# Local attention layers: the sum over the probabilities one place later on VectorE, and PSUM slots given out by expected release

## The reference

```python
for i in range(6):
    x = attn_layer(shift_tokens(x), Wqkv[i], q_scale[i], k_scale[i], Wo[i]) + x
    x = ffn_layer(shift_tokens(x), ln_g[i], ln_b[i], W1[i], b1[i], W2[i], b2[i]) + x
# attn_layer: 16 heads of 64; q, k = l2norm(q) * qs, l2norm(k) * ksc, rotary with a decay;
#   each window of 32 queries attends to its own and the previous 32 keys:
sim = where(mask, -max, einsum('bhwie,bhwje->bhwij', bq, bk2) * 8)
attn = softmax(sim, -1); out = attn @ v; out = out @ Wo
# ffn_layer: layer norm, hg = xn @ W1 + b1; a, gate = split(hg); (a * gelu(gate)) @ W2 + b2
```

## Time and profile before

| | us |
|---|---|
| median of 3 runs | 4151.44 |
| lowest and highest run | 4146.84, 4154.14 |
| the profiled execution, its own time | 4158.42 |
| its span in the trace | 4156.6 |
| stage of the local layers in the trace | 2440 to about 3420 |

### The profile page before, as it was taken

The page is one execution under the profiler, slowest core; times in us unless marked ns, Lnnn a source line. Parts: engine busy times, 40 slices in busy tenths (PEclk is TensorE's granted clock), DMA queues, the critical chain, the costliest instruction groups (busy, mean ns, idle before and its releaser), DMA issues. The chain is left out here.

```text
span 4156.6 us, 96204 instructions
## 1 busy us (share of the span) xinstructions
PE 3506.0 (84%) x40492; PEld 2405.1 (58%) x40492; DVE 2612.0 (63%) x4495; ACT 1970.9 (47%) x3518; POOL 1271.6 (31%) x844
## 2 busy tenths in 40 slices
PE   7575888999999996799778668888888878799996
PEld 4455656777777776433232446666666656466674
DVE  5124485666666663688775857777777757556563
ACT  1132345555555553588711235555555544255552
POOL 1102205555555544100030445555555521000000
PEclk9586799999999997999889779999999999699996
DMA  1022300000000006200001021111111101000000
GB/s 39 5 68 74 124 27 11 9 1 9 1 1 1 1 1 210 95 1 1 4 1 44 24 71 42 34 46 52 34 46 36 27 17 36 12 17 19 11 2 11
DMA packets 88438, 131.27 MB, mean 32 GB/s; under 512 B 18290, under 2 KB 59946, under 8 KB 87244
## 3 DMA queue, kind: packets, MB, share of 16 engines
q1 hardware_dynamic: 85004, 118.89, 10.1%
q0 software_dynamic: 3008, 6.23, 0.4%
HBM read 86.37 MB, written 10.94 MB: 23 GB/s over the span
## 5 line engine op out<-in xcount | busy, mean ns | idle before, releaser
L2196 ACT ACTIVATE narrow_probsT<-narrow_ps_t 128x512 f32<-128x512 f32 (+1 forms) x448 | 233.3, 568 | 224.9 <-PE narrow_ps_t L2110 222.4
L2686 POOL TENSOR_TENSOR wide_probs<-wide_probs,wide_factor 128x1024 f32<-128x1024 f32 x128 | 239.7, 1894 | 311.5 <-ACT wide_factor L2647 311.5
L175 POOL TENSOR_TENSOR model_Y<-model_Y,model_X 128x512 f32<-128x512 f32 x12 | 15.2, 1269 | 1029.7 <-POOLq L66 1029.7
L2643 ACT ACTIVATE wide_probs<-wide_ps_s,wide_nm 128x1024 f32<-128x1024 f32 (+1 forms) x256 | 237.7, 929 | 172.2 <-DVE wide_nm L2728 152.7
L3098 PE MATMUL bonds_ps<-bonds_act_of,bonds_out 128*32 128x448 f32 (+3 forms) x1024 | 284.3, 573 | 25.1 <-ACT bonds_rows L3081 18.6
L2248 DVE TENSOR_REDUCE narrow_part<-narrow_ps_s 128x1 f32<-128x512 f32 x384 | 236.1, 685 | 105.1 <-PE narrow_ps_s L2093 105.1
L3808 POOL TENSOR_TENSOR local_turn<-local_turn 128x1024 f32<-128x1024 f32 x96 | 226.4, 2367 | 225.9 <-DVE local_turn L3866 225.9
L2110 PE MATMUL narrow_ps_t<-narrow_Q,second_KQ 32*128 32x256 f32 (+1 forms) x1664 | 291.5, 410 | 3.0 <-ACT narrow_probsT L2196 3.0
L2093 PE MATMUL narrow_ps_s<-second_KQ 32*128 32x512 f32 x768 | 255.7, 674 | 35.0 <-DMA second_KQ<-narrow_close 16.9
L2723 DVE TENSOR_REDUCE wide_nm<-wide_ps_s 128x1 f32<-128x1024 f32 x128 | 156.0, 1219 | 193.7 <-PE wide_ps_s L2529 193.7
L3047 DVE TENSOR_TENSOR bonds_strain<-peri_in_moved 128x1664 f32<-128x1664 f32 (+3 forms) x128 | 257.5, 2088 | 7.0 <-ACT bonds_act_of L3070 6.0
(11 more groups left out here) (629 smaller groups left out, 8412.9 us busy)
## 6 DMA issues: line engine op xcount, KB each, us to landing
moe_w<-in_L_ffn_w SPq DMA_DIRECT2D x62, 512.0 KB
local_V<-local_V SPq DMA_DIRECT2D x96, 128.0 KB
e_wqkv<-in_L_ffn_qkv SPq DMA_DIRECT2D x6, 1536.0 KB, 7.3
local_V<-local_V SPq DMA_DIRECT2D x144, 64.0 KB
context_rows<-in_ctx SPq DMA_DIRECT2D x8, 768.0 KB
e_keys<-in_ctx_T SPq DMA_DIRECT2D x6, 800.5 KB, 4.5
second_KQ<-narrow_close SPq DMA_DIRECT2D x64, 58.0 KB
e_source<-in_ctx_T SPq DMA_DIRECT2D x4, 800.5 KB, 4.4
```

Source lines behind the costliest of these rows:

```text
L2196: act.activation(probsT[0:high, c % PROBS, h, 0:wide], bank[0:high, 0:wide], ACT.Exp).then_inc(t_taken_act.sem, 1)
L2643: act.activation(probs[:, n % 2, h, lo:hi], ps_s[h][:, 0:hi - lo], ACT.Exp, bias=nm[:, n % 2, h, 2 * half:2 * half + 1], scale=1.0, accum_ ...
L2686: pool.tensor_tensor(v, v, factor[:, n // 4 % 2, j:j + 1].broadcast_to([P, CUT]), ALU.mult).then_inc(lowered[i].sem, 1)
```

## The change

Two edits, both in `local_layers`. First, DVE's part of the step "exp" becomes a step of its own, "inv", which stands just ahead of "s" in both kinds of round; ACT's part of "exp" stays where it is. Second, a slot is no longer `rank % 4`: while the program is built, a small loop walks the units with an assumed time for PE to make each (`MAKES`) and for its reader to be through (`HOLDS`, 1 where none is given), and gives each unit the slot whose last reader is expected to be through first. PE then waits for that slot's last unit. The order of every engine's steps is otherwise the same, and no instruction is added or taken away.

```diff
             if r % 2:
                 ...
                 yield from [("gm", shift), ("k", r), ("pt", r - 2), ("gd", last), ("qt", r - 1), ("sum", r), ("ot", r - 3), ("xs", last),
-                            ("root", r), ("v", r), ("gv", shift), ("s", r - 1), ("rest", r), ("wo", r - 3), ("o", r - 2), ("gx", shift)]
+                            ("root", r), ("v", r), ("gv", shift), ("inv", r - 2), ("s", r - 1), ("rest", r), ("wo", r - 3), ("o", r - 2), ("gx", shift)]
             else:
                 ...
-                            ("s", r - 1), ("rest", r), ("wo", r - 3), ("o", r - 2), ("sh", (r - 4) // 2)]
+                            ("inv", r - 2), ("s", r - 1), ("rest", r), ("wo", r - 3), ("o", r - 2), ("sh", (r - 4) // 2)]
...
+    MAKES = {"q": 2, "k": 2, "v": 2, "kt": 1, "qt": 1, "pt": 1, "ot": 1, "s": 1.5, "o": 1.5, "wo": 2, "gm": 0.5, "gv": 0.5, "ga": 2, "gb": 1, "gd": 1.5}
+    HOLDS = {"q": 4, "k": 4, "ga": 4, "gb": 2}
...
+    slot_of, turn_of, last_in = {}, {}, {}
+    free, users = [0.0] * SLOTS, [[] for _ in range(SLOTS)]
+    clock = 0.0
+    for e in units:
+        k = min(range(SLOTS), key=lambda k: free[k])
+        clock = max(clock, free[k]) + MAKES[e[0]]
+        free[k] = clock + HOLDS.get(e[0], 1)
+        slot_of[e], turn_of[e] = k, len(users[k]) + 1
+        last_in[e] = users[k][-1] if users[k] else None
+        users[k].append(e)
...
         def empty(pe, e):
-            r = rank[e]
-            if r >= SLOTS:
-                wait_taken(pe, units[r - SLOTS])
-            return ps[r % SLOTS], made[r % SLOTS]
+            if last_in[e] is not None:
+                wait_taken(pe, last_in[e])
+            return ps[slot_of[e]], made[slot_of[e]]
...
-                elif kind == "exp":
+                elif kind == "inv":
                     dve.wait_ge(probs_ready.sem, probs_ready.nth(n + 1))
                     dve.tensor_reduce(inv[:, n % 2, :, :].rearrange("p a h -> p (a h)"),
                                       probs[:, n % 2, :, :, :].rearrange("p a h d -> p (a h) d"), AX.X, ALU.add)
```

More of the change, by code:

```diff
@@ L3563, in wait_made @@
         def wait_made(engine, e):
-            r = rank[e]
-            engine.wait_ge(made[r % SLOTS].sem, made[r % SLOTS].nth(r // SLOTS + 1))
+            k = slot_of[e]
+            engine.wait_ge(made[k].sem, made[k].nth(turn_of[e]))
         def full(engine, e):
             wait_made(engine, e)
-            return ps[rank[e] % SLOTS]
+            return ps[slot_of[e]]
         def wait_taken(engine, e):
@@ L3914, in _ @@
                     dve.wait_ge(gelu_ready.sem, gelu_ready.nth(2 * n + 1 + (kind == "gb")))
-                    slot = ps[rank[e] % SLOTS]
+                    slot = ps[slot_of[e]]
                     for j, f in enumerate((0, 1) if kind == "ga" else (2,)):
```

## The result

| | before | after |
|---|---|---|
| median of 4 runs, us | 4149.57 | 4057.05 |
| lowest, highest | 4146.84, 4154.14 | 4045.80, 4061.70 |
| span of the profiled execution | 4156.6 | 4050.6 |
| stage of the local layers in it | 972.7 | 881.5 |

The ratio of the times is 0.9772, with a 95% interval of 0.9747 to 0.9797: 92.5 us less.

A forecast was written before the change was run, and what follows sets the result against it. PE was taken as fullest, idle 85.2 us until DVE evicts q or k; less 24 x (0.75 + 0.25) for new waits and near misses this gave 61 us, so 4090 against 4151.4, range 4067 to 4131.

The forecast's parts named there:

- The two waits: PE idle until DVE has evicted q or k: 44.0 us ahead of transposes, 41.2 us ahead of the gated projection.
- 85.2 - 24 x (0.75 + 0.25) = 61 us: Stage gain: PE's idle time removed, less 0.75 us of new waits and 0.25 of near misses per pair of rounds.
- the new waits: PE per pair of rounds: v 0.5 us for ACT's copy of qt, gd 0.25 us for gm's eviction.
- The charge for near misses: An estimated 0.25 us per pair of rounds for small latenesses elsewhere, such as the mask 0.35 us late.
- The sums: DVE's adding up and inverting of probabilities, 1.71 us, moved into its idle time ahead of the scores, 1.7 on average.
- The pair: An even round and the next odd one on PE: 38.83 us before, forecast at 35.57 us.
- the walk: Hand calculation of one pair of rounds, using PE's distances from the trace without its two idle times.
- the third rival: POOL blocks DVE in the copy sh and gx, losing 1.6 us per pair, 38 us in all: 4128 us; chance 12%.
- The PE-bound one: Neither new wait of PE appears, v and gd find their slots free: 4066 us; chance 8%.
- Half of it: DVE's moved sums aren't hidden in one kind of round, 29 us are lost: 4119 us; chance 15%.
- no change: q's eviction comes as late as before because ACT's squares wait for a late exp: 4151, within 8 us; chance 7%.
- slower: In even rounds v waits for ACT's copy of qt, costing 1.5 us per pair, 36 us: 4187 us; chance 6%.

The follow-up runs named there:

- the fillers: The kernel before with pt's transposes issued twice in even rounds, 4140.42 us (stage 961.2); with kt's also twice in odd rounds, stage 958.0 us.
- the run with qt first: The changed kernel with the step qt moved ahead of ga in even rounds on all engines: median 4083.04 us, stage 903.5 us.
- the second execution: The changed kernel run again, unchanged: median 4074.07 us, stage 887.6 us, ratio to the kernel before 0.978.

## Why the prediction was wrong

*The step that failed* is the sentence "The two waits are the upper bound of this too: nothing below 0, 85 us at most", and behind it the sum "85.2 - 24 x (0.75 + 0.25) = 61 us". It counted what PE loses while it waits, and not what it loses after: the granted clock falls to its lower level behind some of these waits, for about 3.4 us, in which the gated projection took 4.5 us instead of 2.8:

```profile
3020.26 4.51 PE L3723 MATMUL local_ps<-local_centred,e_up 128*128 128x256 f32 x12 [2.48 <-DVE local_turn L3866]
```

The rows had it: 0.97 in the earlier trace rows, which I read as "its full level nearly all the time". Three hundredths of 973 us are 29 us; after the change one hundredth of 882 is left, 9 us. By the record of the granted clock TensorE was at its lower level for 59.3 us of the stage before and for 21.9 us after. 37.4 us less at half speed are 18.7 us of work won back, of the 23.6 by which the busy time fell; the other 4.9 us I can't place. That the waits cause it is shown from both sides: the fillers took stretches away without taking any instruction from a path, from nine to three to one, and the holes of the run with qt first, another kind of idle time, brought three back, each behind a hole of 2.1 us. What decides which of the waits has a stretch behind it isn't shown.

*The terms of the idle time* were nearly right in sum. Of 85.2 us 84.1 went; of the new waits, 18 us were forecast (24 x 0.75), and v for qt, gd for gm and v for gd cost 8.3 + 8.4 + 1.5 = 18.2. That the two agree so well is partly luck: v's wait was put at 12 us and was 8.3, gd's at 6 and was 8.4, and the third was put at none. The charge for near misses (6 us) had nothing behind it: net 67.6 us against a forecast of 61. So of the 30.2 us that the forecast was short in the stage, 6.6 are idle time and 23.6 are PE's busy time, the term that it had at nothing.

*Step by step.* q's eviction was to start 0.15 us after the squares: it does, at 0.14. The sums were to be hidden with nothing to spare: 2.6 us of wait are left ahead of the masks. v was to wait 0.5 us for qt's copy in even rounds: 0.94 in the timeline, 0.4 on average (8.3 in 20); ACT's table load started 0.7 us after pt's copy rather than at once, for it waited for ga. gd was to wait 0.25 us: 0.19. The pair was to take 35.57 us; the one shown took 36.66 (gd at 2798.14 to gd at 2834.80), with 0.4 us more of v's wait, and holes of PE without a releaser of 1.8 us in place of the 1.4 that the walk's rows happened to hold; over the steady part the mean is 35.2 (2 x 17.59, the distance of the updates of Z at L3910).

*POOL beside DVE.* The copy sh has a median of 0.59 us (1.38 in the earlier trace rows), gx one of 1.47 (1.56): the sums did not tie DVE to POOL more than before. By the Trainium skill (SBUF — State Buffer, section "Who interferes with whom") the one that comes second to the shared ports stands for the other's whole instruction. The single executions that stayed long, up to 2.05 and 2.20 us, agree: all 28 over 0.6 us ran beside a product of POOL and ended 0.14 to 0.28 us after it. The worst case, the third rival, did not come.

*The rivals.* The PE-bound one had the size nearly right, 4066, for a wrong reason: the new waits did appear. "Half of it", "no change" and "slower" all need the sums to be late, and they aren't.

## What to carry to other kernels

Where TensorE is the fullest engine, a wait of it of about two microseconds can cost more than its length (here 9 and 12 of 45 did): look at the granted clock in the stretch, and price a mean of 0.97 as up to 3% of the stretch, not as nothing. The upper bound of a gain is then the idle time plus what the lower clock took. Two edits that attack the same wait must be priced together, not added: here 71.5 and 61.1 us alone made 91.2 together. And a hand walk over one pair of rounds with durations from the timeline found both new waits beforehand, and their sum, if by luck, to the microsecond; its blind spot was what isn't a wait for another engine. Where PE has holes that nothing releases, lay the DMA packets of kind "instruction" beside them.

## What was not expected of the hardware

Useless work made a stage shorter: 176 extra matmuls in PE's idle time took 11.5 us off it, through the clock. And PE has holes of its own in every one of these kernels, which end 1.1 to 1.7 us after an instruction packet has landed; their length follows the order of its instructions: moving one group of eight transposes ahead of the gated projection took them from 20.2 us in all (26.1 in the second execution) to 38.2, and cost more than the wait that it removed.
